# Attention written out for all 32 batches in place of a loop over four

## The reference, cut to what matters

```python
q = (query @ Wq + bq).reshape(B, Nq, 16, 16)          # B = 32, Nq = 100
k = (key_value @ Wk + bk).reshape(B, Nkv, 16, 16)     # Nkv = 361
v = (key_value @ Wv + bv).reshape(B, Nkv, 16, 16)
attn = softmax(clip(einsum('bhqd,bhkd->bhqk', q, k) * 0.25, -1e4, 1e4))
x = x + einsum('bhqk,bhkd->bqhd', attn, v).reshape(B, Nq, 256) @ Wo + bo
```

## Time and profile before

| | |
|---|---|
| median of 3 runs | 1663.99 us (1661.3 to 1667.15) |
| the profiled execution | 1657.89 us |
| its span (first to last instruction) | 1656.1 us |
| mean granted TensorE clock | 0.926 |
| TensorE busy | 84% of the span |
| VectorE, ScalarE, GpSimd busy | 64%, 31%, 47% |

### The profile page before, as it was taken

The page is one execution under the profiler, slowest core; times in us unless marked ns, Lnnn a source line. Parts: engine busy times, 40 slices in busy tenths (PEclk is TensorE's granted clock), DMA queues, the critical chain, the costliest instruction groups (busy, mean ns, idle before and its releaser), DMA issues. The chain is left out here.

```text
span 1656.1 us, 33994 instructions
## 1 busy us (share of the span) xinstructions
PE 1392.7 (84%) x9914; PEld 973.8 (59%) x9915; DVE 1054.5 (64%) x2457; ACT 516.9 (31%) x1228; POOL 785.4 (47%) x1072
## 2 busy tenths in 40 slices
PE   4788778877745998989898898989998499999997
PEld 2556545555533776767676676666765266666664
DVE  2687897788731688868788787878886222222221
ACT  1333323332301334434344343434442122222221
POOL 4233552355332457757576576657774122222222
PEclk9899999999875799989899998999996699999999
DMA  4991000000004545545555454555652122222222
GB/s 144 316 319 31 1 1 1 0 0 1 1 12 84 73 91 108 117 90 111 104 106 109 76 115 103 109 101 102 116 109 62 41 46 45 45 45 45 45 46 25
DMA packets 180315, 128.11 MB, mean 77 GB/s; under 512 B 68882, under 2 KB 173090, under 8 KB 180194
## 3 DMA queue, kind: packets, MB, share of 16 engines
q1 hardware_dynamic: 167890, 112.36, 31.2%
q0 software_dynamic: 12304, 14.10, 5.6%
HBM read 36.23 MB, written 44.83 MB: 49 GB/s over the span
## 5 line engine op out<-in xcount | busy, mean ns | idle before, releaser
L1323 DVE TENSOR_REDUCE neg_raw<-bank_s 100x2 f32<-100x722 f32 x256 | 231.1, 903 | 102.2 <-PE bank_s L1539 102.2
L1225 ACT ACTIVATE prob<-bank_st 120x400 f32<-120x400 f32 (+1 forms) x384 | 166.0, 506 | 270.6 <-PE bank_st L1556 270.6
L1880 POOL DMA_INDIRECT out<-result,target x57 | 88.2, 1547 | 266.9 <-DVE result L1854 263.7
L1334 DVE TENSOR_SCALAR bank_st<-bank_st 120x400 f32<-120x400 f32 (+1 forms) x384 | 196.6, 572 | 0.0
L1539 PE MATMUL bank_s<-k_st,q_st 96*100 96x361 bf16 x512 | 137.3, 352 | 55.7 <-issue 20.7
L1080 POOL TENSOR_TENSOR neg_diag<-xident_b,neg_max 100x400 bf16<-100x400 bf16 x128 | 109.2, 853 | 149.9 <-DVE neg_max L1328 140.9
L748 PE MATMUL bank_l<-q_heads,k 128*100 128x192 f32 (+4 forms) x512 | 126.9, 390 | 62.0 <-DVE attn L562 49.8
L1865 DVE TENSOR_TENSOR hidden<-silu,ebank_v 128x512 f32<-128x512 f32 x57 | 39.2, 687 | 196.1 <-PE ebank_v L1789 196.1
L748 PEld LDWEIGHTS bank_l<-q_heads,k 128*100 128x100 f32 x512 | 82.9, 180 | 112.9 <-DVE attn L562 43.5
L396 ACT ACTIVATE q_heads<-q 32x192 f32<-32x192 f32 (+3 forms) x168 | 62.1, 370 | 226.2 <-DVE q L521 217.8
L1547 PEld LDWEIGHTS bank_st<-q_st,k_st 96*120 96x120 bf16 (+1 forms) x1536 | 117.7, 143 | 12.8 <-ACT prob L1225 0.5
(11 more groups left out here) (203 smaller groups left out, 2688.9 us busy)
## 6 DMA issues: line engine op xcount, KB each, us to landing
k_st<-k_part SPq DMA_DIRECT2D x384, 90.2 KB
slot_rows<-empty SPq DMA_DIRECT2D x9, 2967.0 KB, 26.1
q_st<-q_part SPq DMA_DIRECT2D x384, 25.0 KB
kv<-in_ctx_t SPq DMA_DIRECT2D x32, 270.8 KB
expert_w<-in_w SPq DMA_DIRECT2D x16, 512.0 KB, 3.9
rows<-slot_rows SPq DMA_DIRECT2D x57, 129.0 KB, 2.0
residual<-in_w SPq DMA_DIRECT2D x16, 256.0 KB, 4.1
residual<-in_x SPq DMA_DIRECT2D x8, 400.0 KB
```

What stands on the lines that cost most here:

```text
L1225: act.activation(prob[0:KEYS[c], t % 2, c], bank_st[c][0:KEYS[c], 0:4 * T], ACT.Exp).then_inc(exp_done, 1)
L1323: dve.tensor_reduce(neg_raw[:, h:h + 2], bank_s[0:T, :, 0:S], AX.X, ALU.max, negate=True).then_inc(max_done, 1)
L1334: dve.tensor_scalar(tile, tile, CLAMP, -CLAMP, ALU.min, ALU.max).then_inc(clipped, 1)
```

## The change

`every_batch` loses its loop: `body` is called 32 times with plain numbers on each of the five engines. Every count and address becomes a constant; the register instructions and the jump go. The order of work on every engine, the buffers, the waits and what they wait for stay as they are.

```diff
-def every_batch(eng, body):
-
-    for b in range(4):
-        body(b, b, 0)
-    with eng.Fori(1, BATCH // 4 - 1) as i:
-        for q in range(4):
-            body(4 * i + q, q, i)
-    for b in range(BATCH - 4, BATCH):
-        body(b, b % 4, BATCH // 4 - 1)
+def every_batch(body):
+
+    for b in range(BATCH):
+        body(b, b % 4, b // 4)
...
-            every_batch(sp, body)
+            every_batch(body)
...
-            every_batch(pe, body)
+            every_batch(body)
```

More of the change, by code:

```diff
@@ L1173, in body @@
                     diag(b + 1, 0)
-            every_batch(pool, body)
+            every_batch(body)
             last = BATCH // 2 - 1
@@ L1285, in body @@
                         keys_high(b + 2, t - 2)
-            every_batch(act, body)
+            every_batch(body)
             out_copy(BATCH - 1)
@@ L1476, in body @@
                         values(b + 1, 1 - p, 2)
-            every_batch(dve, body)
+            every_batch(body)
             last = BATCH // 2 - 1
```

## The result

The written-out kernel took 1623.74 us in the median of 4 runs (1623.28 to 1625.1); the kernel before 1665.57 us, with the three runs above and one more beside it (1661.3 to 1675.3). The ratio is 0.9742, with a 95% interval of 0.9698 to 0.9786; it is not the quotient of the two medians, which is 0.9749. The profiled execution took 1623.28 us against 1657.89, so 34.6 us less.

A forecast was written before the change was run, and what follows sets the result against it. TensorE bounds the kernel, its loop code refetched at each jump: 21.1 us stalls plus 20.1 half clock less 7.1 q_st waits, 34.1; taken as 33, giving 1625 us profiled, 1631 median with 6 us distance; range 1619 to 1644.

The forecast's parts named there:

- rival A: Attention transfers into q_st don't become late, pairs run at 42.82 us: 42.4 us saved, 1621.6 us; chance 0.10.
- (1): Attention loop: five taken jumps on TensorE and their waits on issue go, saving 21.1 us.
- (2): Attention loop: the half clock on TensorE behind the taken jumps goes, saving 20.1 us.
- Rival C: Attention stall comes from the amount of code TensorE reads, so it stays: 1664 us, no change; chance 0.03.
- Rival B: Half-speed stretches in attention have their own cause, only the jump stalls go: 21.1 us saved, 1643 us; chance 0.06.
- (3): Attention: without stalls TensorE waits for q_st about 1.1 us in each pair of batches, giving back 7.1 us.
- (4): Attention, all engines: register instructions go, SyncE's addresses become constants; at most 0.3 us a pair, possibly nothing.
- (5): Attention, the four engines besides TensorE: new code fetches, some 35 packets on queue 14, taken as zero cost.
- Rival D: Attention code fetches on queue 14 stall their engines: 147 us cost against 41 gained, about 1770 us; chance 0.04.

The follow-up runs named there:

- e1: Attention loop written out on TensorE alone, the other four engines keep it; ratio to the kernel before the change 0.9783 (0.975 to 0.9815).
- e2: Attention loop written out on the four other engines, TensorE keeps its loop; ratio to the kernel before the change 0.9991 (0.997 to 1.0012).
- e4: Written-out kernel with five added stops where TensorE waits for one tiny ScalarE transfer; ratio to the kernel before the change 0.9991 (0.9968 to 1.0013).
- e10: Written-out kernel, TensorE's expert loop body 24 tiles instead of 6, padded with 15 semaphore increments per tile; ratio to the kernel before the change 1.0394.
- e11: Written-out kernel, TensorE's expert loop body 24 tiles instead of 6, padded with 8 semaphore increments per tile; ratio to the kernel before the change 1.0039.
- e5: Written-out kernel, ScalarE instead of SyncE issues all 12 transfers per batch into q_st; ratio to the kernel before the change 0.993 (0.9904 to 0.9955).
- e8: Written-out kernel unchanged, timed again beside the kernel before the change; ratio 0.977 (0.9735 to 0.9805), medians 1618.61 and 1655.17 us.
- e7: Written-out kernel, TensorE's expert loop body 12 tiles instead of 6; ratio to the kernel before the change 0.9766 (0.972 to 0.9812).
- e6: Written-out kernel, TensorE's expert loop body 24 tiles instead of 6; ratio to the kernel before the change 0.9782 (0.9737 to 0.9827).
- e9: Written-out kernel, ScalarE issues six of the 12 q_st transfers per batch, behind the exponentials; ratio to the kernel before the change 0.9698 (0.9665 to 0.9731).

## Why the prediction was right

The direction, the mechanism and the range held: 1623.7 us lies in 1619 to 1644. It lies just under the forecast's own range, 1625 to 1636, and nearer to rival A's 1621.6 than to the 1631 of the forecast. It is the profile that speaks for the forecast and against A: the profiled execution took 1623.28 us, where the forecast had 1625 and A's saving of 42.4 us would have made 1615.5.

**Parts (1) and (2), the stall and the half clock.** I had 21.1 and 20.1 us; the waits on issue that went are 20.7, the busy time 23.1. e1 and e2 showed that they belong to TensorE's loop alone, e4 that the half clock comes with stops of this length without a jump, and e10 against e11 that the jump is slow because the body is too long to be kept. Rival C, which put the stall down to the amount of code read, is out: the written-out kernel reads nearly as much (46 packets on queue 8 in these 26 batches, where before 45 came in the five passes). Rival B is out for the falls behind jumps. Something of it stays: the kernel after has one fall in the middle of the stage, 3.4 us at 0.50 from 689.3 us on, shortly after a wait of 1.34 us for `q_st`; no jump is near. The pair with it is the longest, 44.86 us. Of nine profiles in which TensorE's attention is written out and has no stop put in (not counting e5), e1 and e8 have no such fall in the 26 batches and the other seven have one or two, each next to a wait for `q_st` of 1.3 to 2.0 us; other waits of the same length passed without one. The prediction charged such waits with their length alone.

**Part (3), the transfers.** I expected 1.1 us in each pair, 14 us over these 13 pairs; it was 13.0. Against before 5.8 us more, where I had 7.1. Rival A is out in the profile of the result, where pairs took 43.8 us. In e8's, with pairs of 43.1 and 9.6 us of waits, it is half true; what makes the two differ I don't know. The prediction had no term for VectorE's maxima, which took another 4.7 us back.

**Parts (4) and (5), registers and code.** I put both near zero, and e2 measured them together: 0.9991 (0.997 to 1.0012). Rival D asked for 1.2 us a fetch to decide. With 24 packets more on queue 14, e2's interval leaves at most 2 us of net cost, less than 0.1 us a packet, unless a gain of the same size hides it. In e2 the stops gave the other engines time to catch up. Without stops, e1 has the registers and none of the new fetches, the full change the reverse, and e1's ratio, 0.9783, lies just over the 0.9742 and 0.977 of the full change: no cost of the fetches shows there either.

**What failed.** The sum for the profiled execution, 33 us, was met within 2 (34.6). Its core, the ten pairs behind jumps, gave 33.6 us (their sum before is 470.65 us; the 470.63 of the prediction is a slip that changes nothing). The step that failed is the last one, where I carried the distance of 6 us between the profiled execution and the median over to the new kernel. The written-out kernel has a distance of 0.5 us: 1623.28 profiled, 1623.74 median. The profiled execution of before was at the low end of its kernel's runs; 24 runs of it beside e1 to e4 lay between 1656.07 and 1669.94 with a median of 1664.51. One execution can lie anywhere in such a range, and its place says nothing of where the next kernel's will lie: in e8 it was 3.6 us under the median, in e7 11.4 us over it. Had I left the distance out, the forecast would have been the 1625 us of the profiled execution, but that the median lies so near to it is luck as well.

Why the median fell by 41.8 us where the profiled execution fell by 34.6 stays open. I thought of the stops as what varies from run to run. e4, which has stops and no loop in the attention, had both the level and the width of the loop kernels, but e7 had the width without stops, and the eight runs of e5, with ten falls of the clock in its profile, lay within 4 us. I also expected five to ten packets fewer on queue 8 and some 30 more on queue 14; they were 10 fewer and 25 more.

## What to carry to other kernels

Read the jumps of each engine's loop in the trace: a jump of some 0.2 us is next to free, one of 4 us means that the body is longer than the engine keeps, and then a body shorter by a tenth, which wasn't tried on this loop, should do as well as writing it out; on the other engines the loop cost nothing that e2 could measure. Price a stop of TensorE of some 4 us at its length and about as much again for the half clock. Waits of 1.2 to 2.2 us can bring the half clock too, not each time, and then cost more than they last: in e5 they made most of the loss. When a periodic stall goes, look at what used the time to catch up, here SyncE's issue of small transfers, and give it its own slack.

## What the runs showed of the hardware that I had not expected

TensorE kept a loop body of 1,733 instructions (jump 0.23 us, 7 code packets of about 16 KB for the whole loop) and fetched one of 1,901 again in each pass (3.9 us, 16 packets). A stop of 4.1 us without any jump was followed by 8.4 us at a mean clock of 0.51, the same as behind a jump. A wait of 1.88 us in e6 was followed by some 20 us at half clock, which cost two pairs of batches, together with a short fall ahead of it, some 10 us; in e5 ten falls lay next to waits of 1.2 to 2.2 us. And a second queue, ScalarE's, didn't issue faster than SyncE's: in e9, with both in use, a transfer into `q_st` took ScalarE 0.62 us in the median, as against 0.60 on SyncE, so on these two engines issuing cost the same.
